# Linear attention with rope: the scalar engine's copy of the fourth transposed output, moved ahead of the fourth rope chunk's relu and exp

## The reference

```
q = (x @ Wq.T)                 # 16 heads of 128
k = (x @ Wk.T); v = (x @ Wv.T) # 4 heads of 128, each used by 4 query heads
q = q * cos + _rotate_half(q) * sin      # rope, the same for k
qf = jax.nn.elu(q) + 1.0                 # the same for k: kf
state = state + k_s[..., :, None] * v_s[..., None, :];  z = z + k_s
out   = (q_s @ state) / (q_s . z + EPS)
return out @ Wo.T
```

## Time and profile before

| | us |
|---|---|
| median of 3 runs | 1145.43 |
| lowest and highest run | 1140.72 and 1148.85 |
| span of the profiled execution | 1147.2 |
| PE busy in it | 1036.7 |
| DVE busy | 734.3 |
| ACT busy | 379.3 |
| POOL busy | 225.3 |

### The profile page before, as it was taken

The page is one execution under the profiler, slowest core; times in us unless marked ns, Lnnn a source line. Parts: engine busy times, 40 slices in busy tenths (PEclk is TensorE's granted clock), DMA queues, the critical chain, the costliest instruction groups (busy, mean ns, idle before and its releaser), DMA issues. The chain is left out here.

```text
span 1147.2 us, 16580 instructions
## 1 busy us (share of the span) xinstructions
PE 1036.7 (90%) x5736; PEld 859.6 (75%) x5736; DVE 734.3 (64%) x1657; ACT 379.3 (33%) x731; POOL 225.3 (20%) x284
## 2 busy tenths in 40 slices
PE   6799999999999999999779999878999996999997
PEld 5677778777778777777668888767787875777775
DVE  7655665566566555666549787647788775366465
ACT  4233332333332333333225122134444542322220
POOL 2222221222122122222010100131222224111011
PEclk9999999999999999999999999989999998799999
DMA  9200000000000000000030000020000000000000
GB/s 300 94 1 0 0 0 0 0 0 0 0 0 0 0 0 0 0 0 1 19 123 1 1 1 1 1 93 1 0 0 0 1 2 1 1 15 10 15 14 23
DMA packets 19033, 20.56 MB, mean 18 GB/s; under 512 B 4905, under 2 KB 14898, under 8 KB 18994
## 3 DMA queue, kind: packets, MB, share of 16 engines
q1 hardware_dynamic: 18994, 20.05, 5.4%
HBM read 17.95 MB, written 2.10 MB: 17 GB/s over the span
## 5 line engine op out<-in xcount | busy, mean ns | idle before, releaser
L393 POOL TENSOR_TENSOR rope_sum<-rope_cos,rope_sin 128x512 f32<-128x512 f32 x80 | 113.1, 1414 | 266.6 <-DVE rope_sin L511 266.6
L780 PE MATMUL proj<-wo_sb,attn_out_t 128*128 128x256 f32 x512 | 119.8, 394 | 30.6 <-ACT attn_out_t L416 27.6
L780 PEld LDWEIGHTS proj<-wo_sb,attn_out_t 128*128 128x128 f32 x512 | 99.5, 197 | 48.4 <-ACT attn_out_t L416 30.9
L429 ACT ACTIVATE rope_exp<-rope_sum 128x512 f32<-128x512 f32 x80 | 50.5, 631 | 216.7 <-POOL rope_sum L393 216.5
L729 PE MATMUL num<-v_ones,score_masked 128*128 128x129 f32 x512 | 99.9, 277 | 5.9 <-DVE score_masked L569 5.9
L730 PE MATMUL num<-state,q_t 128*128 128x129 f32 x512 | 99.8, 277 | 0.0
L1751 DVE SCALAR_TENSOR_TENSOR m_acc<-m_expert,gates,m_acc 128x256 f32<-128x256 f32 x128 | 61.9, 484 | 56.7 <-PE m_expert L1830 50.4
L729 PEld LDWEIGHTS num<-v_ones,score_masked 128*128 128x128 f32 x512 | 82.7, 193 | 13.4 <-DVE score_masked L569 8.0
L508 DVE TENSOR_TENSOR rope_cos<-proj,cos_sb 128x512 f32<-128x512 f32 x80 | 55.3, 691 | 57.7 <-PE proj L683 57.7
L1551 PE MATMUL g_ps<-t_u,k_rows 128*128 128x128 f32 x512 | 72.6, 285 | 16.6 <-DVE t_u L1400 16.4
L1551 PEld LDWEIGHTS g_ps<-t_u,k_rows 128*128 128x128 f32 x512 | 63.4, 191 | 30.3 <-DVE t_u L1400 27.8
(11 more groups left out here) (205 smaller groups left out, 2040.4 us busy)
## 6 DMA issues: line engine op xcount, KB each, us to landing
a_stage<-in_wqkv SPq DMA_DIRECT2D x6, 512.0 KB, 5.4
wo_sb<-in_wo SPq DMA_DIRECT2D x1, 2048.0 KB, 9.7
a_stage<-in_wgu SPq DMA_DIRECT2D x4, 512.0 KB, 8.5
out<-x_sb SPq DMA_DIRECT2D x16, 128.0 KB, 1.7
x_sb<-in_x SPq DMA_DIRECT2D x2, 768.0 KB, 11.0
f_wmod<-in_wmod SPq DMA_DIRECT2D x1, 1536.0 KB, 10.1
w_sb<-in_w SPq DMA_DIRECT2D x1, 1280.0 KB
a_wmod<-in_wmod SPq DMA_DIRECT2D x1, 1024.0 KB, 6.2
```

What stands on the lines that cost most here:

```text
L393: pool.tensor_tensor(y[:, parity], t1[:, parity], t2[:, parity], ALU.add).then_inc(s["y_done"], 1)
L780: mm = pe.matmul(proj[:, b, 0:D], o_t[:, i, :], wo[:, i, :], start=(i == 0), stop=(i == H - 1))
```

## The change

ACT's loop over the four output copies issued `e(1 + g)` behind each. Now it does so for g = 0 and 1 only, and `e(3)` and `e(4)` follow behind the loop. So the copy of output 3 stands ahead of `e(3)` and no longer behind it. Nothing else moves.

```
                     for g in range(KVH):
                         drain_turn(c, b, 5 + g, o_t[:, g * REP:(g + 1) * REP, :],
                                    turn[:, bank(5 + g), :].rearrange("p (r t) -> p r t", r=REP))
-                        e(1 + g)
+                        if g < 2:
+                            e(1 + g)
+                    e(3)
+                    e(4)
                     if norm:
```

## The result

The changed kernel is faster. Its median is 1109.65 us (1104.08 to 1110.98, 4 runs) against 1144.85 us in the same set of runs; the ratio is 0.9671, with a 95% interval of 0.9647 to 0.9695 (the two medians alone give 0.969). The kernel before was run again beside each set of experiments; over all its 56 runs its median is 1146.8 us, so the gain is some 35 to 37 us. The forecast was 1108.5 us, with a range of 1103 to 1119.

What follows compares the result with a forecast made beforehand. PE was taken to bound the kernel, idling in the attention loop for ACT's late output copy. Removing 31.8 us of waits and 5.1 us of low clock, 36.9 us in all, gave 1108.5 us, range 1103 to 1119.

Steps and rivals of the forecast that it cites:

- The wait and its cause: In the attention loop, PE's output projection waits for ACT's copy of the transposed output in 15 steps, 27.6 plus 2.2 us.
- The rival that `q_rope(4)` stands behind the copy: The projection really waits for DVE's `rope_sin`, so each step gains only 0.8 us, about 1133 us; chance 0.06.
- the rival "nothing changes": PE's idle time only moves to the next step's transposes, waiting for ACT's k copy; time stays at 1145; chance 0.05.
- The copy early by 0.8 us, covered by `p(5)`: The moved copy ends about 0.8 us before PE's projection; without `p(5)` ahead, PE would wait about 0.7 us.
- The gain per step: Projection starts 2.1 us earlier in 14 steps and 2.4 us in step (7, 0), 31.8 us in sum.
- The lower bound by printed idle times: Counting only PE's printed idle before the projection, 1.97 us a step, 29.8 us in all.
- What the copy pushes back: nothing: On ACT, `e(3)` and `e(4)` still wait for POOL and start as before; the edit costs nothing there.
- the slower rival: Late `out_turn(3)` transposes would hold up `e(3)`, `e(4)` and the `a_h` copy on ACT; 1157 us; chance 0.02.
- The clock: Three loop projections at 1.2 GHz go with the gaps and vanish: 5.1 us more, lower bound nothing.
- The sum: 31.8 us of shorter steps plus 5.1 us of clock give 36.9 us, so 1108.5 us.

Runs made afterwards that it cites:

- late512: The changed kernel with one idle ACT activation of 512 columns (about 0.6 us) ahead of the fourth copy; 1107.49 us, ratio 0.9655 to the kernel before.
- late1536: The changed kernel with one idle ACT activation of 1536 columns (about 1.45 us) ahead of the fourth copy; 1114.91 us, ratio 0.9733 to the kernel before.
- nocover: The changed kernel with PE's `out_turn(3)` put behind `p(5)`, so `p(5)` no longer covers the copy; 1121.36 us, ratio 0.9767 to the kernel before.
- split: The kernel before with the fourth copy put between the relu and the exp of `e(3)`; 1130.85 us, ratio 0.9859 to the kernel before.
- late3072: The changed kernel with one idle ACT activation of 3072 columns (about 2.7 us) ahead of the fourth copy; 1138.27 us, ratio 0.9898 to the kernel before.
- late4x768: The changed kernel with four idle ACT activations of 768 columns ahead of the fourth copy; 1140.27 us, ratio 0.9954 to the kernel before.
- half: The kernel before with the change made only in the steps of b = 0, 8 of 15; 1126.75 us, ratio 0.9821 to the kernel before.
- fill2: The kernel before, ACT order unchanged, with two unread score matmuls on PE ahead of each output projection; 1141.25 us, ratio 0.9962 to the kernel before.
- kgap: The changed kernel with an idle 2560-column ACT activation between the k copy and first q copy of the step; 1147.98 us, ratio 1.0015 to the kernel before.

## Why the prediction was right

**The wait and its cause.** Right. All 15 waits are gone, also the one that the trace had put down to DVE's `rope_sin`. The rival that `q_rope(4)` stands behind the copy is out: in the changed kernel the projection starts at 222.17, while the second half of `q_rope(4)` (`rope_sin`) ends at 222.76 + 0.68 = 223.44. The wait that the rival "nothing changes" pointed at, for the k copy, did not grow: it is 0.3 us in each step.

**The copy early by 0.8 us, covered by `p(5)`.** Right: it ends at 221.33, 0.84 us ahead of the projection. late512 fits into this slack, late1536 does not, and without the cover nocover loses 0.74 us per step where 0.7 was said.

**The gain per step.** The term was mis-sized, by little: 2.1 us was taken, 2.24 was measured. The start of the projection came as forecast (0.70 us behind L686's start in both the estimate and the trace). What I left out is that the projection itself ends sooner after its start when nothing was idle ahead of it: 244.85 - 237.84 = 7.01 us to the next transposes before, 229.08 - 222.17 = 6.91 now. The lower bound by printed idle times (1.97) was too low by 0.27: 0.16 for the records that overlap, which the estimate had, and 0.10 for this. It was too low by the same amount in every run with a gap (the kernel before: 2.24 against 1.97): split 1.58 against 1.31, nocover 0.74 against 0.47, late1536 0.47 against 0.20, late3072 1.75 against 1.48, late4x768 2.03 against 1.76 (period less 31.56, against printed idle). The choice of start-to-start times over printed idle was right, for the reason that the Trainium skill gives (Perfetto Trace Analysis, Tensor Engine Instruction: a matmul's end is estimated); these six pairs put a size on it here.

**What the copy pushes back: nothing.** Right. `e(3)` starts 1.00 us after the start of L686 (222.47 - 221.47) as against 0.99 before, `e(4)` 3.43 against 3.42. DVE waits 3.86 us for the projection; 4.0 was forecast. half shows that a step does not give the gain back. The condition of the slower rival, a late `out_turn(3)`, did not arise: the list of PE's waits has none ahead of these transposes.

**The clock.** Right in sign and size. The three low stretches are gone from the loop, 5.1 us; fill2 measures the term alone at 4.4 us (2.5 to 6.2). The last step keeps one, as said above.

**The sum.** 36.9 us were forecast. The two profiled executions differ by 39.4, of which 0.6 is start-up and 2.0 the mis-sized term (2.2 + 31.6 = 33.8 in place of 31.8). The medians differ by 35.2 in the first set of runs and by 37.2 against all runs of the kernel before. The forecast of 1108.5 lies 1.2 us from the median of 1109.65. That is closer than four runs between 1104 and 1111 us can tell, and a term was 2.0 us short, so this closeness is in part luck; the mechanism and the size of some 37 us are not.

**What stays open.** Why three of the 15 gaps, and not the others of equal length, were followed by a low stretch was not tested. The three of the kernel before are 170.7 us apart (168.58, 339.28, 509.95), every fifth gap, which suggests that it matters when a gap falls and not only how long it is; in kgap they are four and five steps apart. Length seems to count too: split, late3072 and late4x768 had 14 gaps each of 1.3 to 1.77 us and no low stretch behind any of them; the kernel before, half and kgap had 15, 7 and 15 of about 2 us and 3, 2 and 3. The step (7, 1), whose code is the same in all twelve kernels, says the same: 14 of its 21 gaps of 2.05 to 2.36 us were followed by a low stretch, none of its three of 1.60 to 1.83 us. These are counts from one profiled execution of each kernel. How often the clock fell in the other executions, and what the low stretch of the last step costs, are not shown.

## What to carry to other kernels

When an engine's list is in order and two independent pieces stand in it, put first the one whose input is ready first and whose reader is the bottleneck. The test is in the timeline: the engine was idle for a releaser (POOL) that had nothing to do with what PE was waiting for. Check the cover (what the bottleneck does between making the input and needing the copy) and price a wait on PE by starts, not by printed idle. If the granted clock falls at a recurring gap, the gap costs more than its length.

## What the runs showed of the hardware that was not expected

Adding work to PE made the kernel faster (fill2): two extra matmuls per step filled 1.7 of the 1.97 us of the gap, the period stayed, and the time fell by 4.4 us. The clock no longer went to 1.2 GHz in the loop. In the kernel before, a gap of some 2 us was followed by that in 3 of 15 steps. An fp32 matmul of 128x512 takes 0.86 us of PE's stream at 2.4 GHz (eight records in 3.43 us for four matmuls), nearly twice the 0.46 us that the distance between two neighbouring groups of records had suggested.
